# Cross attentions of a two-layer decoder: all four key buffers loaded first, routing logits behind the output products, reciprocals ahead of the residual sums in the drain, the last batch normalised on VectorE

## The reference, cut to what matters

```python
x = x + attention0(layernorm(x))                 # (8, 128, 128) rows, 16 heads
x = x + cross_attention(layernorm(x), ctx)       # layer 0, ctx (8, 77, 96)
x = x + mixture0(layernorm(x))                   # 16 experts, 8 chosen, plus a shared one
x = x + attention1(layernorm(x))
x = x + cross_attention(layernorm(x), ctx)       # layer 1
x = x + mixture1(layernorm(x))                   # 8 experts, 2 chosen

def cross_attention(x, y):                       # 16 heads of 8, 77 keys
    q, k, v = heads(x @ Wq + bq), heads(y @ Wk + bk), heads(y @ Wv + bv)
    w = softmax(q @ k.T * 8 ** -0.5)             # layer 0 clips the scores first
    return join(w @ v) @ Wo + bo
```

## Time and profile before

| | us |
|---|---|
| runs of the kernel before | 562.34, 557.69, 558.77 (median 558.77) |
| the profiled execution, its time | 559.68 |
| its span (first to last instruction) | 557.9 |
| mean granted TensorE clock | 0.918 of full |
| PE / DVE / ACT / POOL busy | 474.1 / 371.1 / 332.8 / 267.3 |

### The profile page before, as it was taken

One profiled execution on the slowest core, in us unless ns is written; L12 is line 12 of the kernel. 1 busy time (PEld: TensorE's weight loads), 2 busy tenths in 40 slices (PEclk: granted clock), 3 DMA queues, 4 the chain that ended last, 5 costly groups with the idle time before them and its releaser, 6 DMA issues. The chain is left out here.

```text
span 557.9 us, 9954 instructions
## 1 busy us (share of the span) xinstructions
PE 474.1 (85%) x3161; PEld 359.8 (64%) x3161; DVE 371.1 (67%) x911; ACT 332.8 (60%) x655; POOL 267.3 (48%) x294
## 2 busy tenths in 40 slices
PE   4689999999578877899994999656689779999995
PEld 3577888876356655688882578444466556777774
DVE  4787777774646745566665476767357454999995
ACT  3687777775446763356552465224467555988883
POOL 1699879777434642466662750113072231745420
PEclk9799999999779995899997899796789969999999
DMA  6614342425255000444332200003580002111101
GB/s 184 210 43 120 101 120 72 126 79 133 71 140 147 1 2 1 136 133 132 116 93 69 58 0 1 0 1 78 139 218 1 2 2 75 33 45 38 38 0 38
DMA packets 34688, 41.80 MB, mean 75 GB/s; under 512 B 5178, under 2 KB 26612, under 8 KB 34420
## 3 DMA queue, kind: packets, MB, share of 16 engines
q1 hardware_dynamic: 33796, 40.65, 26.2%
q10 hardware_dynamic: 848, 0.60, 0.4%
HBM read 30.70 MB, written 8.18 MB: 70 GB/s over the span
## 5 line engine op out<-in xcount | busy, mean ns | idle before, releaser
L1304 POOL TENSOR_TENSOR e_gc<-e_g,e_c 128x512 f32<-128x512 f32 x32 | 41.8, 1309 | 38.1 <-ACT e_g L1287 23.1
L2090 DVE TENSOR_TENSOR e_h_lo<-e_h,e_h_hi 128x512 fp32r<-128x512 f32 x56 | 55.6, 1045 | 3.4 <-ACT e_h_hi L1968 3.4
L1780 POOL TENSOR_TENSOR m_w_hi<-m_w,m_one 128x512 fp32r<-128x512 f32 x16 | 19.7, 1232 | 68.1 <-DMA m_w<-in_L_ffn_W 30.4
L963 ACT ACTIVATE x_pT<-x_turn 77x1024 f32<-77x1024 f32 x32 | 32.7, 1021 | 32.3 <-PE x_turn L901 32.3
L1964 ACT ACTIVATE e_h<-e_h,m_b 128x512 f32<-128x512 f32 x64 | 43.8, 691 | 8.3 <-PE e_h L1864 8.3
L557 ACT ACTIVATE a_p<-xn_all,a_least 128x128 f32<-128x128 f32 x128 | 40.7, 390 | 6.1 <-DVE a_least L596 6.0
L1266 ACT ACTIVATE e_h_hi<-e_h 128x512 fp32r<-128x512 f32 x34 | 21.5, 632 | 33.8 <-DVE e_h L1342 23.9
L901 PE MATMUL x_turn<-consts,x_p 128*77 128x128 f32 x256 | 38.3, 296 | 3.9 <-ACT x_p L968 3.9
L1348 DVE TENSOR_TENSOR e_h_lo<-e_h,e_h_hi 128x512 fp32r<-128x512 f32 x34 | 23.7, 698 | 26.5 <-ACT e_h_hi L1266 26.5
L703 POOL TENSOR_TENSOR a_p<-a_p,a_r 128x512 f32<-128x512 f32 x32 | 33.3, 1042 | 15.0 <-DVE a_r L605 15.0
L901 PEld LDWEIGHTS x_turn<-consts,x_p 128*77 128x77 f32 x256 | 30.3, 158 | 13.4 <-ACT x_p L968 11.1
(11 more groups left out here) (300 smaller groups left out, 1448.2 us busy)
## 6 DMA issues: line engine op xcount, KB each, us to landing
e_c<-spread SPq DMA_DIRECT2D x32, 256.0 KB, 3.3
x_ks<-kstack SPq DMA_DIRECT2D x16, 462.0 KB, 5.5
kstack<-a_blk_hi SPq DMA_DIRECT2D x32, 154.0 KB, 3.1
m_w<-in_L_ffn_W SPq DMA_DIRECT2D x16, 256.0 KB, 3.1
a_raw<-in_experts SPq DMA_DIRECT2D x17, 192.0 KB, 2.5
kstack<-a_blk_lo SPq DMA_DIRECT2D x16, 154.0 KB, 2.9
su_reversed<-scratch SPq DMA_DIRECT2D x1, 1024.0 KB, 5.6
w_wkv<-in_L_attn_Wkv SPq DMA_DIRECT2D x1, 1024.0 KB, 7.6
```

The source lines that it names most:

```text
L963: act.activation(pT[k % 2][:, :, :], tb[0:NKV, :, :], ACT.Copy).then_inc(S["turned_out"], 1)
L1304: pool.tensor_tensor(gc[k % 2][:, :], g[u % 2][:, :], c[k % NC][:, :], ALU.mult).then_inc(S["weighted"], 1)
L2090: dve.tensor_tensor(h_lo[half][f][:, :], h[half][f], h_hi[half][f][:, :].bitcast(F32), ALU.subtract).then_inc(S["lo_done"], 1)
```

## The change

SP issues the keys of four batches before anything else, instead of two first and two between the two parts of the queries. On PE the logits of batches 0 to 4 are no longer one piece ahead of the output product of batch 6: those of 0 and 1 stand in step 17, those of 2 to 4 in step 19 behind the output product of batch 6, that of 5 in step 21 behind the output product of batch 7. On DVE the reciprocal and scaling (now `finish`) stand ahead of the residual sum in steps 17 and 19, and as before behind it in steps up to 15. The normalised rows of batch 7 are made by DVE in place of POOL, which still makes `rstd`.

```diff
--- before.py
+++ after.py
@@ -796,8 +796,8 @@
                 def keys(b):
                     sp.dma_start(ks[b % KEYS][:, :, :].bitcast(F32), kstack[l, b]).then_inc(S[f"ks_landed{b % KEYS}"], 16)
 
-                keys(0)
-                keys(1)
+                for b in range(KEYS):
+                    keys(b)
                 for j in range(2):
                     at, to = later_part(j)
                     landed = S[f"qs_landed{j}"]
@@ -806,9 +806,6 @@
                         for g in range(4):
                             sp.dma_start(qs[32 * part:32 * part + 32, g, to].bitcast(F32),
                                          src[32 * g:32 * g + 32, at].bitcast(F32)).then_inc(landed, 16)
-                    if j == 0:
-                        for b in range(2, KEYS):
-                            keys(b)
                 if loads is not None:
                     loads(sp)
                 for b in range(KEYS, B):
@@ -910,8 +907,8 @@
                         for hg in range(4):
                             mm = pe.transpose(bk[:, P * hg:P * hg + P], oS[b % 2][:, P * hg:P * hg + P], ident)
                         mm.then_inc(S["back_done"], 1)
-                    if ahead is not None and n >= STEPS + 2 and n % 2 == 0:
-                        for b in range(0 if n == STEPS + 2 else n // 2 - 5, n // 2 - 4):
+                    if ahead is not None and (n > STEPS and n % 2 == 1 or n == 2 * SLOTS + 4):
+                        for b in {STEPS + 1: (0, 1), STEPS + 3: (2, 3, 4), 2 * SLOTS + 4: (7,)}.get(n, (n // 2 - 5,)):
                             pe.wait_ge(S["xT_out"], since["xT_out"] + b + 1)
                             ahead.logits(pe, b, tb)
 
@@ -989,6 +986,15 @@
                                              in1=q_hi[:, at].bitcast(F32), op0=ALU.add,
                                              op1=ALU.subtract).then_inc(S["q_lo_out"], 1)
 
+                def finish(b):
+                    dve.wait_ge(S["back_done"], since["back_done"] + b + 1)
+                    dve.reciprocal(r[:, :], back[:, :, DH]).then_inc(S["recip_done"], 1)
+                    dve.wait_ge(S["recip_done"], since["recip_done"] + b + 1)
+                    if b >= 2:
+                        dve.wait_ge(S["slot_done"], since["slot_done"] + b - 1)
+                    dve.tensor_tensor(o[b % 2][:, :].rearrange("p (h d) -> p h d", d=DH), back[:, :, 0:DH],
+                                      free(r[:, 0:1], [[1, H], [0, DH]]), ALU.mult).then_inc(S["normed"], 1)
+
                 first_low(0)
                 first_low(1)
                 for n in range(2 * B + 8):
@@ -1009,6 +1015,8 @@
                                               ALU.max).then_inc(S["scores_read"], 1)
                         else:
                             dve.tensor_reduce(m[n % 2][:, :, :], scores(n), AX, ALU.max).then_inc(S["max_done"], 1)
+                    if n > STEPS and batch_at(n, 5) is not None:
+                        finish(batch_at(n, 5))
                     b = batch_at(n, 7)
                     if b is not None:
                         dve.wait_ge(S["y_done"], since["y_done"] + b + 1)
@@ -1034,15 +1042,12 @@
                         dve.wait_ge(S["aggr_done"], since["aggr_done"] + b + 1)
                         dve.tensor_scalar(var[:, b:b + 1], mv[:, b, 1:2], LN_EPS, None,
                                           ALU.add).then_inc(S["var_done"], 1)
-                    b = batch_at(n, 5)
-                    if b is not None:
-                        dve.wait_ge(S["back_done"], since["back_done"] + b + 1)
-                        dve.reciprocal(r[:, :], back[:, :, DH]).then_inc(S["recip_done"], 1)
-                        dve.wait_ge(S["recip_done"], since["recip_done"] + b + 1)
-                        if b >= 2:
-                            dve.wait_ge(S["slot_done"], since["slot_done"] + b - 1)
-                        dve.tensor_tensor(o[b % 2][:, :].rearrange("p (h d) -> p h d", d=DH), back[:, :, 0:DH],
-                                          free(r[:, 0:1], [[1, H], [0, DH]]), ALU.mult).then_inc(S["normed"], 1)
+                    if b == B - 1:
+                        dve.wait_ge(S["rstd_done"], since["rstd_done"] + B)
+                        dve.tensor_scalar(xn_all[:, b, :], x_all[:, b, :], mv[:, b, 0:1], rstd[:, b:b + 1],
+                                          ALU.subtract, ALU.mult).then_inc(S["xn_done"], 1)
+                    if n < STEPS and batch_at(n, 5) is not None:
+                        finish(batch_at(n, 5))
                     if ahead is not None and n == 2 * B + 4:
                         ahead.low_half(dve, 0)
                 if ahead is not None:
@@ -1067,6 +1072,7 @@
                         pool.wait_ge(S["var_done"], since["var_done"] + b + 1)
                         pool.tensor_tensor(rstd[:, b:b + 1], var[:, b:b + 1], eps_pow[:, b:b + 1],
                                            ALU.pow).then_inc(S["rstd_done"], 1)
+                    if b is not None and b < B - 1:
                         pool.wait_ge(S["rstd_done"], since["rstd_done"] + b + 1)
                         pool.tensor_scalar(xn_all[:, b, :], x_all[:, b, :], mv[:, b, 0:1], rstd[:, b:b + 1],
                                            ALU.subtract, ALU.mult).then_inc(S["xn_done"], 1)
```

## The result

| | before | after |
|---|---|---|
| median of the runs, us | 560.84 (20 runs, 557.69 to 564.91) | 557.98 (20 runs, 554.78 to 560.14) |
| ratio to before, 95% interval | | 0.9946 (0.9927 to 0.9965) |
| profiled execution, us (span) | 559.68 (557.9) | 554.78 (553.0) |
| mean granted clock of PE | 0.918 | 0.918 |

The gain is 3.0 us (2.0 to 4.1). The forecast was 553.6 us, in a range from 551.2 to 557.0, and the measured 557.98 lies above it. Two things missed. The kernel before had been shown with three runs, median 558.77; in twenty it is 560.84, so 2.1 us of the miss of 4.4 are the starting point. The other 2.3 are the gain (2.9 us between the medians, for 5.2). The profiled execution of after is the fastest of its twenty: its distance from that of before (4.9 us) is larger than the change's effect. So the two traces serve for the order and length of single steps and not for the sum.

A forecast was written before the change was run, and what follows sets the result against it. A chain of waits, neither engine nor bandwidth, was taken to bound the kernel. Keys 0.7 + 0.5, drains 2.4 + 2.0, clock -0.4 sum to 5.2 us: 558.77 - 5.2 = 553.6 us, range 551.2 to 557.0.

The forecast's parts named there:

- Keys, layer 1, 0.7: Second cross attention: early keys win 3.0 us in step 4, 1.1 kept at step 8, 0.7 after the clock.
- 0.4 taken off for the clock: Layer 1: half-speed work moves from step 4 to step 8, costing 0.4 of the 1.1 us kept.
- cold step 8: Rival: layer 1 keys give -0.2, clock behind drains costs 1.5; 3.2 us gained; 0.25 together with "half the drain".
- Keys, layer 0, 0.5: First cross attention: step 4's 0.70 us wait for keys goes, worth 0.5 us, between 0.2 and 0.9.
- Drain, layer 0, 2.4: End of first cross attention: reordered logits, reciprocals and last rows gain 2.4 us, between 1.3 and 2.7.
- First term 1.7: Layer 0 drain: earlier reciprocal of batch 7 and fewer logits ahead bring the copy `oT` 1.7 us earlier.
- Cost 0.1: Layer 0 drain: two logits newly ahead of the slot of batch 6 cost 0.1 us.
- Drain, layer 1, 2.0: End of second cross attention: same reordering gains 2.0 us, between 1.1 and 2.3; `oT` 1.25 earlier, POOL limits again.
- Clock behind the drains, -0.4: Both mixtures' starts: PE's clock rise need not move along with earlier drains; 0.4 us lost, from -1.5 to +1.5.
- half the drain: Rival: batch 6's slot later or PE's queue limits; drains give 1.3 + 1.1, total 3.2 us; 0.25 with "cold step 8".
- Keys wait removed whole: Rival, layer 1: keys(4) land much earlier, clock stays full, step 4's 3.0 us are kept; 551.3 us; chance 0.10.
- The slower one: Rival: both mixtures' starts run longer at 1.2 GHz; slower once the rise comes 12 us later in the work; chance 0.05.

The follow-up runs named there:

- keys_only: Kernel before with only the keys of four batches issued first; ratio 0.9981 to the kernel before, -1.1 us.
- drain_only: Kernel before with the whole change except the keys, which are issued as before; ratio 0.9951 to the kernel before, -2.7 us.
- splits_only: Changed kernel with GpSimd's four pairs of expert-weight splits placed one by one behind the rows of batches 0 to 3, second attention; 0.9939 of the kernel before.
- key4_first: Changed kernel with keys of batch 4 issued ahead of the experts' loads in the second cross attention; ratio 0.9951 to the kernel before.
- logits_later: Changed kernel with logits of batches 2, 3, 4 moved from step 19 to step 21; ratio 0.9958 to the kernel before.
- warm_head: Changed kernel with twenty unneeded identity products in steps 2 and 3 of each cross attention; ratio 0.9917 to the kernel before.
- head_before: Kernel before with twenty unneeded identity products in steps 2 and 3 of each cross attention, no part of the change; ratio 0.9996.
- warm: Changed kernel with twelve unneeded identity products in each cross attention's drain, in TensorE's gaps; ratio 0.9906 to the kernel before.
- drain_warm: Kernel before with the drain's part of the change and twelve unneeded identity products in each drain, keys as before; ratio 0.9902.
- recip_only: Kernel before with only reciprocal and scaling moved ahead of the sums in the drain; ratio 0.9973, -1.5 us.

## Why the forecast missed, step by step

- **The starting point.** Three runs gave 558.77, twenty 560.84. The prediction took the profiled execution's 559.68 and then went by the lower median. Twenty runs spread over 7.2 us, and the median of three of them can lie 2 us off. This is 2.1 of the 4.4 us, and it is luck of the draw and no mechanism.
- **Keys, layer 1, 0.7.** The step "PE sits idle until keys(2)", with 3.0 won in step 4, was right (3.16), and so was "then step 8 decides" with 1.1 won there (1.0 in the mean of the table above). In the trace of after it is 2.3: SP reached the loads 0.9 us earlier but keys(4) only 0.1, since one issue for `m_b` took 1.28 us there, and they landed in 4.5 us, not 6.6. That landing is this execution's. The step that failed is the **0.4 taken off for the clock**: the two steps behind step 8 cost 1.7 us more in the mean. By step 10 the term is about -0.8 and at the turning back of batch 6 -0.6, below even the lower end of its range (-0.2). "The whole penalty of 1.3", read from steps 4 and 5, was too small a bound: steps 8 to 10 took 4.79 us at full clock and up to 7.31 without. The times don't resolve the term: keys_only gained 1.1 us (2.4 to -0.3), and beside the drain the keys gave 0.3. The rival "cold step 8" had the mechanism.
- **Keys, layer 0, 0.5.** Not resolved. Step 4's wait went, yet step 6 stands at 29.49 us after and 29.48 in drain_only (29.69 before), with the clock low over steps 4 and 5 in all three. In keys_only it stands at 27.43, with the clock back before step 6. Over the eight traces with the keys first and the seven with those of before, leaving out the kernels with fillers at the head, the means are 29.69 and 30.11, in a spread of 4.3. The term took a wait's length as won although the work on its other side may be cold.
- **Four keys delay keys(0): nothing.** Right: the first scores of layer 1 come 7.99 us into the stage before and after.
- **Drain, layer 0, 2.4.** 1.8 in the pair of traces, 1.9 in the mean. "First term 1.7" failed: `o` was ready at 207.31 as said, but the three logits ahead of its turning took 1.30 us, not 0.7, at the lower clock, which had come at 206.2. `oT` came 2.88 us behind the start of the turning back in place of 3.85, a gain of 1.0. "Cost 0.1" failed too: the two logits ahead of the slot of batch 6 cost 0.3, and that slot came 0.47 us late, over the 0.3 that the prediction had named as a sign of being wrong. "0.6 more" held (0.33 us from `oT` to the output product, 0.95 before). The last rows brought their whole 0.5 (3.03 us from the output product to the last turning, 3.53 before), because GpSimd's batch 6 wasn't the limit that was reckoned: 1.0 - 0.3 + 0.6 + 0.5 = 1.8. With the same drain and a clock that falls later, splits_only shows what the term would be:

```profile
204.22:214.97 10.75, 6.26 (x55) 4.77 (x53) 4.97 (x20) 5.67 (x12) 3.62 (x5) 0.89 0.00 1
```

```profile
202.54:214.32 11.78, 8.24 (x54) 6.39 (x53) 5.05 (x20) 5.66 (x12) 3.66 (x5) 0.65 0.00 1
```

  The first is splits_only at a granted clock of 0.89, 10.75 us; the second is after at 0.65, 11.78 us. The 0.6 us that this term missed are 0.7 at `oT` and 0.2 at the slot, less the 0.3 that the last rows brought beyond what was reckoned.
- **Drain, layer 1, 2.0.** 2.3 in the pair of traces, 2.4 in the mean. Here the clock fell at 441.7, behind the three logits (0.73 us). `oT` came 1.5 us earlier behind the turning back of batch 7 (1.78 us for 3.32), where 1.25 was forecast; the two logits cost 0.3 again; and GpSimd's batch 6 did limit, with 1.12 us of waiting for it at 444.11, so that the last rows brought 0.1.
- **Clock behind the drains, -0.4.** The chain after, at the first products of the second mixture, against the earlier trace rows: 0.43 us each until 451.75, then 0.23.

```profile
451.32 0.43 PE e_h L1870
451.75 0.38 PE e_h L1868
452.12 0.23 PE e_h L1869
```

  From the mixtures' first product to the rise, before (two rows) and after (two rows):

```profile
216.53:221.20 4.67, 4.67 (x11) 3.70 (x12) 3.42 (x20) 2.48 (x4) 0.00 (x0) 0.50 0.02 4
453.05:456.70 3.65, 3.65 (x10) 2.88 (x10) 3.27 (x16) 2.91 (x4) 1.42 (x2) 0.50 0.01 2
```

```profile
214.32:219.83 5.51, 5.50 (x13) 4.36 (x14) 3.57 (x21) 3.14 (x5) 0.00 (x0) 0.50 0.01 3
447.54:451.94 4.40, 4.40 (x11) 3.47 (x11) 3.92 (x19) 3.07 (x5) 1.42 (x2) 0.50 0.02 6
```

  The rise did not move along with the earlier end: 0.84 and 0.75 us more at half speed, at 0.45 us each 0.7 us lost. In other traces the time at half speed at a mixture's start is 3.3 to 6.0 us. Its mean is 0.5 us (layer 0) and 0.6 us (layer 1) longer with the change's drain (after, drain_only, key4_first, logits_later, splits_only, warm_head) than with that of before (before, keys_only, head_before), which makes 0.5 us lost. So the term was about right.
- **Sum.** By means of traces: -0.6 + 0.4 + 1.9 + 2.4 - 0.5 = 3.6 us, inside the 2.0 to 4.1 measured; the forecast's was 5.2. Of the 1.6 between them 1.3 are the keys of layer 1, that is, the clock behind step 8. warm and drain_warm show by the time that cold work in and behind the drains has a price. For step 8 the price is read from traces, and no run kept its clock up with all else the same. That each of these falls was caused by the change isn't shown: they lie at other points in other executions.
- **Rivals.** Of the 25 in 100 given to "half the drain" and "cold step 8", the second names the mechanism. Both gave 3.2 us, close to the 3.0 measured, but by luck: the second has 4.4 for the drains (4.3 in the means) and then 1.5 for the clock behind them (0.5 measured), the first has 2.4 for the drains. The slot of batch 6 was late as "half the drain" has it, yet the drains were not halved. "Keys wait removed whole" needed what key4_first lacked: keys(4) early and GpSimd's splits out of the way. The slower one is far off: the rise came under 1 us later, 12 were needed.
- **Chances.** "Faster by over 1%: 0.37" is a little more than its parts give: less than half of 0.50 and nearly all of 0.10 make at most 0.35.

The Trainium skill, TensorE: Matmul & The Clock Gate, section HAM oscillation, has the work behind a wait for DMA start cold; the prediction weighed it and stayed above it. Step 8 agrees with it (4.79 us of waiting, then 0.85 for the scores), and step 10 puts the term where the rule did, at its lower end or below. A wait for DMA of 1.23 us, in drain_only's step 8, left the clock at 1.00.

## What to carry to other kernels

Price a wait with the clock that the work behind it gets. A stretch of idle time that is moved can take its cold work along, and here the traces lose about as much behind step 8 as the keys had won in it. When a removed wait brings nothing, look for the engine that was hidden by it (GpSimd's splits behind the keys) and remove both at once: edits that gave nothing each gave 3 to 6 us together. Where idle time of the bound engine can't be removed, unneeded products in it can pay (2 to 4 us here), but a trace has to show that the granted clock then stays up: the same fillers on the kernel before cost 6 us. And read a step's length from several traces of the same code, since one pair can mislead: after and before differ by 1.8 us at the turning back of batch 6 in layer 1, and the means over their orders of keys by 0.6 the other way.

## What the runs showed of the hardware that was not expected

The stretch from the first mixture's start to the second cross attention holds the same instructions in every kernel here (662 matmuls), and its length differs by 5 us. Its window in drain_warm and in recip_only:

```profile
217.26:375.69 158.43, 136.51 (x662) 103.42 (x662) 101.09 (x316) 73.75 (x144) 66.22 (x79) 0.93 0.22 65
```

```profile
217.63:381.30 163.67, 141.73 (x661) 106.65 (x659) 101.09 (x319) 73.66 (x144) 66.30 (x79) 0.90 0.22 63
```

VectorE, ScalarE and GpSimd are busy for the same time; TensorE is busy 5.2 us longer at a clock of 0.90 in place of 0.93. So an edit's effect on a trace can be hidden by how long the clock is low 100 us later, and one trace of each kernel can't weigh an edit of 1 us. The Trainium skill, TensorE: Matmul & The Clock Gate, Part 1: The HAM clock gate, calls the watching free-running, not tied to the kernel's start, with the same kernel differing from run to run. The traces agree: layer 0's instructions and their order are the same in after and in key4_first, and the clock fell 14.6 us into the stage in the one and 18.9 in the other.

What stays open: why warm_head's and head_before's 2.6 to 3.2 us in layer 0 reach the time by half and not at all. The traces put the rest into longer stretches behind, but one execution of each doesn't tell whether the fillers bring these. For the same reason the distance between drain_only's 2.7 us (1.3 to 4.1) and the 4.1 by which its two drains are shorter than before's isn't assigned beyond the 0.5 of the clock behind them.
